# Two-layer Perceiver on one core: split first chunk and PSUM maxima in the last cross-attention head, other filler counts, and a reordered expert loop

## The chip, the cores and the metric

The kernel runs on one core of a Trainium2 chip. The metric is the time of one execution in device microseconds (us), lower is better; the figure that counts is the median of several executions. A core has five engines with queues of their own: PE (matrix products, results in PSUM), DVE (VectorE, elementwise and reductions), ACT (ScalarE, activations and copies), POOL (GpSimd, which here also issues some transfers) and SP (SyncE, which only issues transfers). They wait for each other through semaphores, and each runs its own instructions in order.

## The reference, cut to what matters

`x` is 256 tokens by 512, `ctx` 4096 by 512. Six residual steps follow one another, each on a layernorm of `x`:

```python
x = x + xattn0(ln(x), ctx)      # 16 heads of 128, 4096 keys
x = x + attn0(ln(x))            # 16 heads of 32, q, k, v rounded to e4m3
x = x + ffn0(ln(x))             # relu MLP plus a gated expert
x = x + xattn1(ln(x), ctx)      # keeps the 54 largest scores of a token
x = x + attn1(ln(x))            # 16 heads of 32, biases
x = x + moe(ln(x))              # 64 experts, top 8, at most 64 tokens each
```

The cross-attention and the last step, where most of the change lies:

```python
scores = einsum('bqhd,bkhd->bhqk', q, k); attn = softmax(scores)
ctx_out = einsum('bhqk,bkhd->bqhd', attn, v) @ Wo
h = silu(xg @ w1.T) * (xg @ v1.T)      # per expert, F = 192
y = h @ w2;  out = scatter_add(weight * y)
```

## The kernel before, in words

Every engine has one function per step, and the order of work on each is written out by hand. There is no scheduler; the order in the code is the order in the queue.

**Cross-attention.** A head's 4096 keys are worked through in 8 chunks of 512 (`NCH`), numbered over all heads as `n = h * NCH + j`; `TAIL` is the first chunk of the last head. Per chunk PE makes scores into the two-bank PSUM tile `twin`, ACT copies them into `S` in SBUF (`store_scores`), DVE keeps a running maximum (`keep_max`). After the last chunk DVE folds it (`L692`), POOL takes the maximum over partitions (`largest_score`, L896) into `mrow`. Then, per chunk, DVE subtracts (`shift`, L699), ACT takes the exponential (`raise_scores`, L539) and rounds it to a high part (`round_e`, L548), DVE makes the low part (`split_e`, L719), and PE multiplies both with the values (`weigh`, L403, and for the last head the sums, L408). The parts have two places, so `round_e` of a chunk waits until the chunk two before it is weighed. In all heads but the last this lies beside the projection of the next head's keys. In the last head there is nothing beside it, and `stay_awake` (L135), products into a bank that nobody reads, fills PE's wait. POOL also loads the values back from HBM in `load_v`.

**Attentions.** `tensor_attention` works in four groups of four heads: scores, maxima on DVE (`maxima`, L1262), the negated maxima split in three and turned (L1049), scores turned (L1062, L1066), exponential on ACT (L1199), sums and products (`weigh_group`, L1084, L1092), `normalise` on DVE, and at the end `project_out(i, c)` (L1099) for token tile `i` and group `c`. In the first attention q, k and v are quantised on DVE before (L1255 ends q and k each). It calls `stay_awake` 30 times before the first scores.

**Experts.** Two experts make a pair, 32 pairs, two pairs a couple `q`, four pairs a group. Weights lie in a ring of 7 pairs (2304 KB each); SP refills a place once `hid_down` says that the couple is done. For the first group the tokens are gathered by products (`gather`); for the later ones `find_gates(g)` yields the token numbers of the group, `gpsimd_rows` fetches the rows by an indirect transfer (L1854), and `turn_rows` transposes them into `GATHER_B` (L1915), from which ACT copies (`move_rows`). Then `up` (L1930), silu on ACT, `make_hid` on DVE, `turn` (L1943), `move_hid` on DVE, `down` (L1954, L1958), `round_y` on ACT, `split_y` and `make_selT` on DVE and `spread_out` (L1968) into the two output banks. A loop pass of PE is: up, gates of the next group (every other pass), up, turn rows, down, two spreads, turn, turn rows.

## Time and profile before

| | |
|---|---|
| runs | 1680.07 us median of 3 (1679.98 to 1680.2) |
| the profiled execution | 1675.72 us, its span 1673.9 us |
| PE busy | 1624.5 us, 97% of the span, 9280 products |
| DVE, ACT, POOL busy | 1076.1, 695.1, 127.0 us |
| transfers | 270.40 MB, mean 162 GB/s |
| TensorE's granted clock | 0.996 on average over the span |

The profile is one execution, so durations and gaps are those of 1675.72 us, 4.35 us under the median of the runs. Busy PE includes the filler products. The cross-attention ends at about 1180 us of the span, the first attention at about 1250, the experts start at about 1456.

### The profile page before, as it was taken

The page shows a single profiled execution, that of the slowest core. Times are in us where ns is not written, and L with a number is a line of the kernel's source. Part 1 is how long each engine was busy: PE and PEld are TensorE (multiplying, and loading weights), DVE is VectorE, ACT ScalarE, POOL GpSimd, SP SyncE. Part 2 cuts the span into 40 slices and gives each one's busy share as a digit, 9 for nine tenths or more (in the row PEclk, how much of TensorE's full clock was granted, in tenths as well). Part 3 has the DMA queues.
Part 4 walks back from the last instruction along what each step waited for, and adds up shares of the span by engine and source line. Part 5 has one row for each costly group of instructions (what it writes and reads, how often), then busy time and mean ns, then how long its engine had stood idle before and what let it go on. Part 6 is the DMA issues. An engine that isn't in the chain of part 4 may idle for free.

```text
span 1673.9 us, 23515 instructions
## 1 busy us (share of the span) xinstructions
PE 1624.5 (97%) x9280; PEld 1285.7 (77%) x9280; DVE 1076.1 (64%) x1706; ACT 695.1 (42%) x938; POOL 127.0 (8%) x212
## 2 busy tenths in 40 slices
PE   8998999999999999999999999999979999999998
PEld 7887888888788888878888888888747746554444
DVE  4445777777777777777777779998473842633333
ACT  3334544454444444454454546665231321322222
POOL 0000000000000000000000010111000000011110
PEclk9999999999999999999999999999989999999999
DMA  6755445554454545545544552325210517479994
GB/s 225 202 173 167 123 130 141 130 133 116 140 140 127 133 127 132 132 139 139 135 131 118 139 147 92 108 95 193 91 54 30 201 51 304 171 208 426 422 422 174
DMA packets 117292, 270.40 MB, mean 162 GB/s; under 512 B 7168, under 2 KB 76992, under 8 KB 111040
## 3 DMA queue, kind: packets, MB, share of 16 engines
q1 hardware_dynamic: 96512, 194.45, 36.7%
q0 software_dynamic: 20672, 74.46, 14.5%
q8 instruction: 74, 1.21, 0.3%
q14 instruction: 34, 0.28, 0.0%
HBM read 200.69 MB, written 68.19 MB: 161 GB/s over the span
## 4 chain that ended last, share of the span: by engine, by line
PE 71%; issue 16%; DVE 6%; DMA 3%; ACT 2%; POOL 2%; SPq 0%; DVEq 0%; POOLq 0%; ACTq 0%
PE bank L390 16%; PE bank L41 16%; PE bank L362 12%; PE bank L403 7%; PE bank L1930 4%; PE bank L1554 3%; PE bank L1968 2%; PE bank L1954 2%; DMA v_dram<-v_out 1%; DVE e_lo L719 1%; PE bank L135 1%; PE bank L428 1%; PE bank L1958 1%; POOL v_back L890 1%; PE bank L1915 1%
## 5 line engine op out<-in xcount | busy, mean ns | idle before, releaser
L719 DVE TENSOR_TENSOR e_lo<-S,e_hi 128x1024 fp32r<-128x1024 f32 x128 | 156.6, 1224 | 89.3 <-ACT e_hi L548 88.7
L362 PE MATMUL bank<-cT_hi,wk_hi 128*128 128x512 f32 x512 | 205.4, 401 | 0.0
L390 PE MATMUL bank<-wv_hi,cT_hi 128*128 128x512 f32 x512 | 199.8, 390 | 3.4 <-DVE wv_lo L656 3.4
L539 ACT ACTIVATE S<-S 128x1024 f32<-128x1024 f32 x128 | 135.6, 1059 | 160.2 <-DVE S L699 159.6
L362 PE MATMUL bank<-cT_hi,wk_lo 128*128 128x512 f32 x512 | 200.6, 392 | 0.0
L390 PE MATMUL bank<-wv_hi,cT_lo 128*128 128x512 f32 x512 | 199.4, 390 | 0.0
L362 PE MATMUL bank<-cT_lo,wk_hi 128*128 128x512 f32 x512 | 199.2, 389 | 0.0
L390 PE MATMUL bank<-wv_lo,cT_hi 128*128 128x512 f32 x512 | 199.2, 389 | 0.0
L548 ACT CAST e_hi<-S 128x1024 fp32r<-128x1024 f32 x128 | 134.7, 1052 | 139.6 <-PE bank L403 135.1
L712 DVE TENSOR_TENSOR esum<-esum,S 128x512 f32<-128x512 f32 x210 | 145.0, 691 | 71.1 <-ACT S L539 67.5
L403 PE MATMUL bank<-e_hi,v_back 128*128 128x256 f32 x880 | 167.0, 287 | 5.3 <-DVE e_lo L719 3.5
L687 DVE TENSOR_TENSOR mx<-mx,S 128x512 f32<-128x512 f32 x224 | 154.4, 689 | 14.3 <-ACT S L533 10.4
L699 DVE TENSOR_TENSOR S<-S,mrow 128x1024 f32<-128x1024 f32 x128 | 155.3, 1216 | 3.2 <-POOL mrow L896 3.2
L41 PE MATMUL bank<-q_hi,k_hi 128*128 128x256 f32 x512 | 145.4, 284 | 10.2 <-DVE k_lo L674 10.2
L403 PEld LDWEIGHTS bank<-e_hi,v_back 128*128 128x128 f32 x880 | 138.8, 191 | 9.5 <-issue 7.9
L41 PE MATMUL bank<-q_lo,k_hi 128*128 128x256 f32 x512 | 144.8, 283 | 0.0
L41 PE MATMUL bank<-q_hi,k_lo 128*128 128x256 f32 x512 | 144.8, 283 | 0.0
L519 ACT CAST k_hi<-bank 128x512 fp32r<-128x512 f32 x128 | 75.3, 588 | 155.2 <-PE bank L362 155.2
L533 ACT COPY S<-bank 128x1024 f32<-128x1024 f32 x128 | 128.7, 1006 | 11.1 <-PE bank L41 11.1
L890 POOL DMA_DIRECT2D v_back<-v_dram x110 | 59.0, 537 | 868.0 <-PE bank L403 832.0
L403 PE MATMUL bank<-e_lo,v_back 128*128 128x256 f32 x440 | 124.4, 283 | 0.0
L724 DVE TENSOR_TENSOR v_out<-bank,v_out 128x512 fp32r<-128x512 f32 x112 | 76.9, 687 | 59.9 <-ACT v_out L555 59.9
(279 smaller groups left out, 2805.2 us busy)
## 6 DMA issues: line engine op xcount, KB each, us to landing
w<-in_w_moe SPq DMA_DIRECT2D x32, 2304.0 KB, 17.5
v_dram<-v_out SPq DMA_DIRECT2D x112, 512.0 KB, 4.6
v_back<-v_dram POOLq DMA_DIRECT2D x110, 512.0 KB
v_dram<-v_back SPq DMA_DIRECT2D x16, 512.0 KB, 3.9
ctx_nat<-in_ctx SPq DMA_DIRECT2D x8, 1024.0 KB, 4.9
ctx_raw<-in_ctxT SPq DMA_DIRECT2D x7, 1024.0 KB, 8.0
v_late<-v_dram POOLq DMA_DIRECT2D x14, 512.0 KB
l_w_qkv<-in_l_wqkv SPq DMA_DIRECT2D x6, 1024.0 KB, 5.5
```

What stands on the lines that cost most here:

```text
L41: last = e.matmul(dst, lhs, rhs, start=(n == 0), stop=(n == len(terms) - 1))
L362: t = e.matmul(banks[b][:], l, r, start=(c == 0 and m == 0), stop=(c == DT - 1 and m == 2))
L390: t = e.matmul(banks[b][:], l, r, start=(c == 0 and m == 0), stop=(c == DT - 1 and m == 2))
L403: t = e.matmul(banks[O_BANK][:, 0:T], v[:, i, l, :], r[:, i, :], start=(j == 0 and i == 0 and m == 0), stop=(j == NCH - 1 and i == CT - 1 ...
L533: e.copy(S[:, j * CT:(j + 1) * CT, :].rearrange("p a t -> p (a t)"), twin[:]).then_inc(s_stored, 1)
L539: e.activation(Sj, Sj, ACT.Exp).then_inc(raised, 1)
L548: e.copy(e_place(n)[0][:], S[:, j * CT:(j + 1) * CT, :]).then_inc(e_rounded, 1)
L687: own.done(e.tensor_tensor(mx[:], mx[:], two, ALU.max))
L699: e.tensor_tensor(Sj, Sj, mrow[:].unsqueeze(1).to_broadcast([P, CT, T]), ALU.subtract).then_inc(shifted, 1)
L712: e.tensor_tensor(esum[:], esum[:], two, ALU.add).then_inc(e_summed, 1)
L719: e.tensor_tensor(lo[:], Sj, hi[:].bitcast(F32), ALU.subtract).then_inc(e_split, 1)
L724: e.tensor_tensor(place_of[:, :, 1, :].bitcast(F32R), banks[b][:].rearrange("p (q d) -> p q d", q=HPQ), place_of[:, :, 0, :].bitcast(F32), ...
```

## The change

**Last head of the cross-attention.** DVE folds the first seven chunks' maxima while PE still makes the last scores, reduces the last chunk straight from `twin`, and joins the two (`keep_last_max`). ACT stores the last scores only behind that. Chunk `TAIL` goes through shift, exponential, rounding and split in two halves (`HALVES`), and PE's `weigh` starts on the first. The sum fold and the ones matrix move behind the maxima, `add_head` of the head before goes from the middle of the loop to its end, each `shift` goes ahead of the split before it. POOL issues the loads of chunks `TAIL` + 2 and + 3, then the maximum, then the load of `TAIL` + 1. `weigh` of the very last chunk signals once behind the products and once behind the sums. The filler goes from 18 calls to 6.

**First attention.** 30 calls become 19; 3 are added between the two parts of the first scores, 7 ahead of the second and third group's scores, and the 4 ahead of the turned maxima of three groups go. In both attentions token tile 0 has its four output products before tile 1's second.

**Experts.** The filler of the router goes from 10 calls to 3 in the second tile and from 7 to 2 behind the ranks. `gather` waits for each half of the selection. Gates go into the bank of the second y instead of `GATHER_B`, so `find_gates` waits for `y_split` and `down` for `gates_moved`. The first passes are written out: `down(0)` comes ahead of `turn_rows(4)`. In the later passes `turn_rows(2q+2)` stands ahead of the second `up` (and, in passes with gates, right behind them). The last `down` comes behind three more spreads and DVE moves hid first in the last pass. The output tile 0 is added before tile 1's last spread is done.

```diff
@@ tensor_cross
-            stay_awake(e, banks[K_BANK], 18)
+            stay_awake(e, banks[K_BANK], 6)
@@ scalar_cross
             h = XH - 1
+            move_o(h - 1)
             store_scores(h, NCH - 1)
-            move_o(h - 1)
-            for j in range(NCH):
+            for m in HALVES:
+                raise_scores(h, 0, m)
+                round_e(h, 0, m)
+            for j in range(1, NCH):
                 raise_scores(h, j)
                 round_e(h, j)
             move_o(h)
             e.wait_ge(sum_ready, h)
+            e.wait_ge(weighed, NH + 1)
@@ vector_cross
+            def keep_last_max():
+                own.wait(e)
+                e.wait_ge(max_ready, XH - 1)
+                own.done(e.tensor_reduce(mxr[:], mx[:].rearrange("p a t -> p t a"), AX.X, ALU.max))
+                own.wait(e)
+                e.wait_ge(scored, NH)
+                own.done(e.tensor_reduce(mx[:, 0, :], twin[:].rearrange("p (a t) -> p t a", t=T), AX.X, ALU.max))
+                own.wait(e)
+                e.tensor_tensor(mxr[:], mxr[:], mx[:, 0, :], ALU.max).then_inc(max_folded, 1)
...
             h = XH - 1
+            keep_last_max()
+            fold_sum(h - 1)
             own.done(e.tensor_scalar(ones_r[:], ident[:], 0.0, 1.0, ALU.mult, ALU.add))
-            fold_sum(h - 1)
-            keep_max(h, NCH - 1)
             own.wait(e)
-            shift(h, 0)
+            for m in HALVES:
+                shift(h, 0, m)
+            invert_sum(h - 1)
             shift(h, 1)
-            invert_sum(h - 1)
-            for j in range(NCH):
+            for m in HALVES:
+                split_e(h, 0, m)
+            for j in range(1, NCH):
+                if j + 1 < NCH:
+                    shift(h, j + 1)
                 split_e(h, j)
-                if j == NCH // 2:
-                    add_head(h - 1)
-                if j + 2 < NCH:
-                    shift(h, j + 2)
+            add_head(h - 1)
@@ gpsimd_cross
-                        for ahead in (1, 2, 3):
-                            load_v(n + ahead)
+                        load_v(n + 2)
+                        load_v(n + 3)
+                        largest_score(h)
+                        load_v(n + 1)
@@ tensor_attention
-                if k == 0 and f < 3:
-                    stay_awake(e, turned_bank(0), 4)
...
-                stay_awake(e, W_BANK, 30)
+                stay_awake(e, W_BANK, 19)
                 e.wait_ge(quant_done, 2)
                 scores(0, (0, 1, 2))
+                stay_awake(e, W_BANK, 3)
                 scores(0, (3,))
...
+                    if f < 2 and k == 0:
+                        stay_awake(e, W_BANK, 7)
                     scores(f + 1, (0, 1, 2))
...
             project_out(0, 1)
-            project_out(1, 1)
             project_out(0, 2)
             project_out(0, 3)
+            project_out(1, 1)
             project_out(1, 2)
@@ tensor_moe
-                stay_awake(e, banks[5], 2 + 8 * i)
+                stay_awake(e, banks[5], 2 + i)
...
-            stay_awake(e, GATHER_B, 7)
+            stay_awake(e, GATHER_B, 2)
...
+            up(0)
+            find_gates(1)
+            up(1)
+            up(2)
+            turn(0)
+            up(3)
+            down(0)
+            turn_rows(4)
+            turn(1)
+            turn_rows(5)
+            for q in range(2, COUPLES):
+                up(2 * q)
+                if q % 2 == 0 and q // 2 + 1 < NG:
+                    find_gates(q // 2 + 1)
+                if 2 * q + 2 < PAIRS:
+                    turn_rows(2 * q + 2)
+                up(2 * q + 1)
+                down(q - 1)
+                if q == COUPLES - 1:
+                    turn(q)
+                spread_out(2 * q - 4)
+                spread_out(2 * q - 3)
+                if q < COUPLES - 1:
+                    turn(q)
+                    turn_rows(2 * q + 3)
+            spread_out(PAIRS - 4)
+            down(COUPLES - 1)
+            for p in range(PAIRS - 3, PAIRS):
+                spread_out(p)
@@ scalar_moe
+                    silu(2 * q)
+                    if q > 1 and 2 * q + 2 < PAIRS:
+                        move_rows(2 * q + 2)
+                    silu(2 * q + 1)
+                if q == 1:
+                    move_rows(4)
                 if q:
                     round_y(2 * q - 2)
+                if q == 1:
+                    move_rows(5)
+                if q:
                     round_y(2 * q - 1)
```

## Rows read from the trace of the kernel before

**Rows 1.** Chain that ended last (start us, us, what), end of the last head

```profile
1176.52 0.38 ACT oT L561
```

**Rows 2.** Timeline, last head (start, us, engine, line, operation, count, idle before)

```profile
1147.95 0.69 DVE L692 TENSOR_REDUCE mxr<-mx 128x256 f32<-128x512 f32 x1
...
1148.98 1.03 POOL L896 PARTITION_ALL_REDUCE mrow<-mxr  x1
...
1150.11 2.36 DVE L699 TENSOR_TENSOR S<-S,mrow 128x1024 f32<-128x1024 f32 x2 [1.46 <-POOL mrow L896]
...
1152.51 1.05 ACT L548 CAST e_hi<-S 128x1024 fp32r<-128x1024 f32 x1
...
1153.59 1.23 DVE L719 TENSOR_TENSOR e_lo<-S,e_hi 128x1024 fp32r<-128x1024 f32 x1 [1.04 <-ACT e_hi L548]
...
1168.73 0.48 PE L403 MATMUL bank<-e_hi,v_late 128*128 128x256 f32 x2 [0.96 <-DVE e_lo L719]
```

**Rows 3.** Timeline, first attention

```profile
1211.02 1.23 DVE L1255 SCALAR_TENSOR_TENSOR l_k<-l_xn,l_qkT 128x1024 bf16<-128x1024 f32 x1
...
1214.84 1.89 DVE L1262 TENSOR_REDUCE l_mx<-bank 128x2 f32<-128x512 f32 x3 [1.46 <-PE bank L1037]
...
1229.06 1.94 PE L1084 MATMUL bank<-l_eT,ones 128*32 128x256 f32 x16
...
1235.39 1.07 PE L1084 MATMUL bank<-l_eT,ones 128*32 128x256 f32 x16
```

**Rows 4.** Windows of the first attention (PE, PEld, DVE, ACT, POOL busy, PEclk, DMA, GB/s)

```profile
1214.40:1217.50 3.10, 0.70 (x8) 0.14 (x8) 2.60 (x8) 0.30 (x1) 0.00 (x0) 1.00 0.80 327
1217.50:1224.40 6.90, 4.32 (x37) 2.88 (x40) 6.59 (x13) 4.41 (x7) 0.00 (x0) 0.50 0.01 3
```

**Rows 5.** Timeline, end of the second attention and the router

```profile
1449.96 5.42 PE L1099 MATMUL bank<-l_w_out,xT 128*128 128x512 f32 x12
1451.12 0.42 DVE L1287 SCALAR_TENSOR_TENSOR xT<-bank,l_inv 128x256 f32<-128x256 f32 x1
...
1459.14 2.45 PE L135 MATMUL bank<-ident 128*128 128x128 f32 x20
...
1459.79 1.04 ACT L2034 CAST xn_hi<-xn 128x1024 fp32r<-128x1024 f32 x1 [0.23 <-DVE xn L123]
```

**Rows 6.** Waits of PE from 1470 us to the end (total us, times, longest)

```profile
PE bank L1954 <- DVE hidT L2108: 1.9, 1, 1.9
PE bank L1915 <- DMA rows<-xn_dram,ids: 1.4, 1, 1.4
PE bank L1943 <- DVE h L2101: 1.0, 1, 1.0
PE bank L1968 <- DVE selT L2087: 0.9, 1, 0.9
PE bank L41 <- DVE sel L2064: 0.6, 1, 0.6
```

**Rows 7.** One group of four pairs, as a window

```profile
1572.28:1596.61 24.33, 24.33 (x144) 12.02 (x146) 8.45 (x24) 6.01 (x12) 3.79 (x4) 1.00 1.01 424
```

**Rows 8.** Chain that ended last, in the expert step

```profile
1649.81 5.31 PE bank L1930 x32
...
1662.10 1.94 PE bank L1954 x8
1664.03 1.02 PE bank L1958 x8
...
1667.99 2.09 PE bank L1968 x8
...
1670.10 0.69 DVE x L2167
```

**Rows 9.** The tile rows6, from 1476 us to the end: issues and landings

```profile
L1854 POOL DMA_INDIRECT rows<-xn_dram,ids x28: 943/947/1189, 1477.7 to 1626.9; - x28
...
DMA to landing us min/median/max: 8.7/11.8/13.1
```

More of the change, by code:

```diff
@@ L226, in k_before, with of_chunk, reached @@
             return n if n <= LATE * NCH + NCH else n - 1 if n > LATE * NCH + NCH + 1 else 0
+        HALVES = (0, 1)
+        def of_chunk(j, m=None):
+            return slice(j * CT, (j + 1) * CT) if m is None else slice(j * CT + m * CT // 2, j * CT + (m + 1) * CT // 2)
+        def reached(n, m=None):
+            return n + 1 + (n > TAIL or n == TAIL and m != 0)
         def e_place(n):
@@ L397, in weigh @@
                 e.wait_ge(landed_v, value)
-                e.wait_ge(e_split, n + 1)
+                e.wait_ge(e_split, n + 1 if n <= TAIL else reached(n))
                 if j == 0 and h:
@@ L401, in weigh @@
                 for i in range(CT):
+                    if n == TAIL and i == CT // 2:
+                        e.wait_ge(e_split, reached(n))
                     for m, (l, r) in enumerate(((0, high), (1, high), (0, low))):
@@ L404, in weigh @@
                                      start=(j == 0 and i == 0 and m == 0), stop=(j == NCH - 1 and i == CT - 1 and m == 2))
+                if n == NH - 1:
+                    t.then_inc(weighed, 1)
                 if h == XH - 1:
@@ L910, in gpsimd_cross @@
                     elif n == TAIL:
[L911 to L912 removed]
+                        load_v(n + 2)
+                        load_v(n + 3)
+                        largest_score(h)
+                        load_v(n + 1)
                     elif n + 3 < NH:
                         load_v(n + 3)
[L915 removed]
+                    if h and j == 0 and n != TAIL:
                         largest_score(h)
@@ L1008, in sync_attention @@
                 if k == 0:
-                    e.wait_ge(e_split, NH - NCH + 2 * n + 2)
+                    e.wait_ge(e_split, reached(TAIL + 2 * n + 1))
                 else:
@@ L1887, in gather @@
                 if c == 0:
-                    e.wait_ge(sel_made, TT)
                     e.wait_ge(xn_split, 1)
                 cols = slice(c * P, (c + 1) * P)
-                matmuls(e, gather_bank(c), [(xn[:, i, cols], sel[:, 0, i, :]) for i in range(TT) for xn in (xn_hi, xn_lo)]).then_inc(gathered, 1)
+                for i in range(TT):
+                    if c == 0:
+                        e.wait_ge(sel_made, i + 1)
+                    for part in (xn_hi, xn_lo):
+                        t = e.matmul(gather_bank(c), part[:, i, cols], sel[:, 0, i, :], start=(i == 0 and part is xn_hi),
+                                     stop=(i == TT - 1 and part is xn_lo))
+                t.then_inc(gathered, 1)
             def find_gates(g):
@@ L1901, in find_gates @@
                     e.wait_ge(gates_moved, 3 * g)
-                    e.wait_ge(xg_moved, DT + GROUP * (g - 2) + 2 if g > 1 else DT)
+                    e.wait_ge(xg_moved, DT)
+                    if g > 1:
+                        e.wait_ge(y_split, GROUP * (g - 1) - 2)
                 for n in range(GROUP):
@@ L1969, in spread_out @@
                                      start=(p == 0 and part is y_hi), stop=(p == PAIRS - 1 and part is y_lo))
+                    if p == PAIRS - 1 and i == 0:
+                        t.then_inc(spread, 1)
                 t.then_inc(spread, 1)
@@ L2020, in move_rows, with silu @@
                 e.copy(xgT[:, p % 2].rearrange("p c s -> p (c s)"), GATHER_B).then_inc(xg_moved, 1)
+            def silu(p):
+                e.wait_ge(hid_up, p + 1)
+                if p >= 2:
+                    e.wait_ge(hid_made, 2 * (p - 1))
+                e.activation(sa[:, p % 2, :], banks[UP_BANKS[p % 2]][:, 0:FF], ACT.Silu).then_inc(hid_silu, 1)
             def round_y(p):
@@ L2161, in vector_moe @@
                 if q < COUPLES:
-                    move_hid(q)
+                    if q not in (0, COUPLES - 1):
+                        move_hid(q)
                     if q % 2 and q // 2 + 2 < NG:
                         make_sel(q // 2 + 2)
-            e.wait_ge(spread, PAIRS)
             for i in range(TT):
+                e.wait_ge(spread, PAIRS + i)
                 e.tensor_tensor(x[:, i, :], banks[OUT_BANKS[i]][:], x[:, i, :], ALU.add).then_inc(y_added, 1)
```

64 lines of the change are left out of this document (23 added, 41 removed).

## The prediction

> **What bounds the kernel now.** I read the shares of the page first: PE is busy 97% of the span, so a gain can only come from PE's waits and from busy time that is filler. Then the chain of waits, to see which stretches are not plain PE work, then the timeline of those stretches, then the waits of PE by releaser. The reader is to see that the change leaves the long loop of heads alone (span 0 to 1142) and works on four places where PE waits or fills: the last head, the first attention, the router, and both ends of the expert loop. In the middle of the expert loop PE is busy all 24.33 us of a group of four pairs [rows 7]; nothing is to be had there, and the transfers run beside it at full share too.
>
> **Last head.** Before, ACT stores the last scores (1.0), DVE takes them in two steps of 0.7 and folds from 1147.95 to 1148.64, so the scores themselves end at about 1145.45; POOL reduces from 1148.98 to 1150.01, because its three loads hold it until then [rows 2]. After: DVE folds the first chunks beside the last scores, then reduces `twin`. The trace has no reduction of 1024 columns; one of 512 takes 0.69 in SBUF [rows 2] and three from PSUM take 1.89, 0.63 each [rows 3]. By twice 0.63 it takes 1.25; were PSUM read with a stride of 256 twice as slow, 2.5; and 0.63 is the least that half the columns take, so no gain is below that. I take 1.25, since the PSUM rows, which read in a straight line, show no extra. The join is 256 columns, 0.35 by half of 0.69. Maximum ready at 1145.7 + 1.25 + 0.35 = 1147.35, POOL done at 1148.45. DVE has by then folded the sums and made the ones. Shift in halves (0.6 each, half of 2.36 for two [rows 2] and again halved): the first is out at 1149.15. ACT's four halves, 0.55 to 0.6 each by halves of 1.05, end at 1151.7; DVE's split of the first half waits for its own `shift(h, 1)` until 1151.2 and ends at 1151.85. PE starts there instead of at 1154.9, when the split of 1153.59 was done [rows 2]: 3.0 earlier. PE's filler: the fold of the sums is later now, so PE's output products end at 1150.55, and 6 calls of 0.22 (20 products, 10 calls, 2.45 [rows 5]) end at 1151.9. Filler and wait match; 18 calls would have held PE until 1154.6.
> The second chunk gives 0.9 back: its rounding stands behind the four halves, its split ends at 1155.2, PE would be free at 1154.3. From there both kernels go by the same circle, a chunk weighed, rounded 1.05, split 1.22, two chunks in 5.1. `add_head` inside the loop made a wait of 0.96 [rows 2]; at the end it is hidden by the last products. 3.0 - 0.9 + 1.0 = 3.1, and I find 0.3 more where the restarts of PE fall away: 3.4. The early signal lets ACT move `oT`, 0.38 [rows 1], beside the sums: 0.4. **3.8** in all. The load of chunk `TAIL` + 1 moves behind POOL's reduction, 1.4 later; it is wanted only at 1155.2, 6.7 after its issue.
>
> **First attention.** DVE is free at 1213.4 and waits 1.46 for the first scores, PE being in its filler until about 1214.4, although k was ready at 1212.25 (1211.02 + 1.23) [rows 3]. 11 calls less end at 1211.9, so PE waits for k and DVE starts 1.45 earlier. From here I followed each engine's list with the durations of the trace. Where it wins most is behind the second split of maxima: before, the filler of 4 calls stood between the maxima and their turning and took 2.07 because the clock had fallen; the 7 calls now stand ahead of scores that wait for DVE anyway. The sums of the first group (1229.06 before) start at 1225.4 and, at full clock, last 1.07 instead of 1.94; those of the second group (1235.39 before) start at 1230.6 [rows 3]. That is 4.7, with the clock up.
> The clock is the open term. Before, PE was busy 0.70 of 3.1 us, at full clock, and the stretch that follows has 0.50, 1.2 GHz [rows 4]. In the new order PE is busy some 0.8 of 3.6 us between the second filler and the turned scores, about as little. With the whole stretch at 1.2 GHz my lists give 2.6 instead of 4.7. I take **4.0**, between, since the new order has one such thin place and the old one had several.
> The Trainium skill speaks against taking filler away ("TensorE: Matmul & The Clock Gate", on the clock gate: throttled is the default state and activity lifts it). By it the fall would remain and the 2.6 stand; the trace shows the fall in the same place, and cannot show the new order.
>
> **Output order.** Six products take 5.42, 0.9 each [rows 5]. Tile 0's last is the third instead of the fourth, starts at 1449.96 + 1.8 = 1451.8, and its input is moved at 1451.54 [rows 5]: not late. DVE's add, norm and all behind it come 0.9 earlier, in both attentions: **1.8**. Tile 1's end is the same 5.42, and DVE comes to it later than that.
>
> **Router.** Tile 1 is normalised at 1459.76, but the 10 calls hold PE until 1461.4; ACT is free for the move at 1460.83 [rows 5]. With 3 calls the move starts there instead of at 1462.06: 1.2. With `gather` starting on the first half of the selection (the filler of 7 would cover that start, 2 don't) two products of 0.23 are done before the second half: 0.5. **1.7.** PE stays busy for most of this stretch, so I expect no fall of the clock; if it fell over the gather, 16 products of 0.23 would double, 3.6.
>
> **Start of the experts.** PE waits 1.0 for the first hid, 1.4 for the first row transfer, 0.6 for the third selection [rows 6]. Written out, up(1) and up(2) cover the first wait. From the gates of group 1: three ups (half of 5.31 each), a turn of 0.33, `down` 1.94 + 1.02 [rows 8]: 11.4 us, and the rows landed 10.9 behind these gates. So `down(0)` ends 3.1 earlier. But now both row moves of ACT stand ahead of the two roundings of y, so split, selection and `find_gates(2)` end later behind `down(0)`: I get 1.2 of waiting there (0.6 before), and 0.4 for rows 5. `down(1)` starts 1.3 earlier. Bounds: all three waits gone, 3.0; rows late, 0. I take **1.3**. The Trainium skill says that transfers of all issuing engines run on the same 16 DMA engines and interleave ("DMA: Bandwidth & Descriptors", Issuing engines are not separate DMA queues). By it the weights that `down(0)` now releases earlier would share with rows 5 to 7, which before had landed by then, and the term would go towards 0.
>
> **In the loop.** The gates bank is free in time (the y of that bank is split before the selection is made), so that wait costs nothing; without that cover it is one split, 0.7. A group's first row is wanted earlier: from the end of `find_gates` 14.3 before, 11.7 now, one up less. Gates moved and issued take 1.0 and landing 8.7 at least, 11.8 in the median, 13.1 at most [rows 9]. The group's first is issued into the least queue, and the first of group 1 took 9.4, so 10.4 < 11.7: nothing.
>
> **End of the experts.** From the end of the last up (1655.12) to the end of the adds (1671.5) 16.4 [rows 8]. PE waits 1.9 and 0.9 [rows 6]. After: down(14), turn, two spreads of 1.02 until 5.1, spread(28) from 5.75 (its y rounded and split), down(15) from 6.75 to 9.7, spread(29), then spread(30) from 11.45 and (31) to 13.5, each behind rounding 0.6, split 0.7, selection 0.3. The first add starts half a spread earlier; adds end at 14.4: **2.0**.
>
> **Sum.** 3.8 + 4.0 + 1.8 + 1.7 + 1.3 + 2.0 = 14.6. Nothing else of the span changes its order, and the transfers of the later steps are issued by signals that move along. The profiled execution's 1675.72 (span 1673.9 and 1.8 around it) becomes 1661.1; the runs are 4.35 above it, which I keep: 1680.07 - 14.6 = **1665.5**.
>
> **The rivals.** (a) The clock: it stays at 1.2 GHz through the first attention, and falls once more where filler was taken. For it: the thin stretch [rows 4]. Against: the head's and router's fillers shrink only by waits. 14.6 - 1.4 - 3.6 = 9.6, 1670.5; with the first alone 1666.9. (b) The reduction from PSUM is slow and the start of the experts gives nothing, because the rows share with the weights: 14.6 - 1.25 - 1.3 = 12, and waits that my lists miss (each engine's list has some twenty hand-overs of 0.04) take 3 more: 1671. (c) Slower: rows of a group's first pair too late. PE then stands still once per group, in six groups. Each us that the landing takes over 10.7 costs 6 us. At the median 11.8 it costs 6.6, 1672; at 13.1, 14.4, and all is lost, 1680; slower from 13.8 on. For it: the loop's transfers are at full share [rows 7]; against: only the later rows of a group queue behind others. (d) The fillers were never on the path, and only the reordering counts: 1.45 and 1.2 go, 1668.
>
> **How the numbers follow.** Forecast with (d) and the milder half of (a) 0.73, the rest of (a) 0.10, (b) 0.08, (c) 0.09, of which 0.03 beyond no change. 0.2% is 3.4 us, about what a measurement of this kernel can tell from no change. Low: all waits at the start gone (+1.7) and the clock up (+0.7) give 1663.1, and I leave 0.6 for smaller ones; high: 1671.5 takes in (b) and the larger (a). Faster 0.94, same 0.03, slower 0.03.
>
> **What would show it.** PE's first product of the last head near 1152 and the move of `oT` ahead of the last sums; the reduction from `twin` at 1.25; granted clock of the first attention's stretch; `down(0)` ending before row 4 is turned; a wait of PE for the selection of about 1.2, and none at L1915 in the later groups. I am wrong if L1915 waits for rows six times, or if a new stretch has 0.50.

## The result, and the profile after

The changed kernel takes 1664.01 us (median of 4 runs, 1663.39 to 1668.64), against 1680.03 us (4 runs, 1677.14 to 1680.2) for the kernel before on the same chip: a ratio of 0.9915, 95% interval 0.9894 to 0.9935, so faster by 10.9 to 17.8 us. The forecast was 1665.5 (range 1662.5 to 1671.5): faster, as forecast, 1.5 us beside the number. Run again beside experiments 5, 6 and 8 the changed kernel gave 1664.65 (6 runs) against 1679.33 (11 runs) for the kernel before, 14.7 us less.

The profiled execution took 1663.39 us. Top of its page, span and busy time by engine:

```profile
span 1661.6 us, 23410 instructions
PE 1619.7 (97%) x9220; PEld 1281.3 (77%) x9220; DVE 1076.4 (65%) x1708; ACT 695.5 (42%) x940; POOL 126.8 (8%) x212
```

The busy share tells nothing of the change: PE was 97% busy before too, with its filler counted in. So the account is made by stages, each from the start of one instruction to the start of another that both kernels have (the last one to the end of the adds), from the two profiled executions (us):

| stage | before | after | gain |
|---|---|---|---|
| last `v_back` load to the last maximum on POOL | 5.84 | 4.39 | 1.45 |
| from there to the first `rstd` of the next norm on POOL | 32.77 | 30.50 | 2.27 |
| first attention (third reduction of `l_sc` to the next norm's first `rstd`) | 36.61 | 33.89 | 2.72 |
| from there to the first norm behind the second attention | 205.60 | 204.75 | 0.85 |
| router (second norm to the first issue of rows) | 19.12 | 17.16 | 1.96 |
| start of the experts (to `find_gates(2)`) | 17.20 | 15.98 | 1.22 |
| five periods of a group | 5 x 24.33 | 5 x 24.09 | 1.2 |
| last `find_gates` to the end of the adds | 54.83 | 53.29 | 1.54 |

Together 13.2. The spans differ by 12.3, since the long loop, which no edit touches, happened to be 0.91 longer in the execution of after. Over the 14 kernels profiled here the last `v_back` load stands anywhere from 1143.14 (the kernel before) to 1147.82, with the same code ahead of it. The execution of before that the prediction was read from was the quickest of all in that stretch. Part of the wandering is the clock: in the first 160 us of the span it was at 0.50 for no time in two of them (before, and experiment 10), for 3.4 us in seven and for 6.8 us in five; the load stands at 1143.14 and 1144.42 in these two, at 1144.05 to 1145.82 with 3.4 us, and at 1145.40 to 1147.82 with 6.8. The medians differ by 16.0, more than the two spans; what the executions without a trace did in that loop isn't known, so I compare stages from here on.

**Last head.** Timeline, as in [rows 2]:

```profile
1146.66 1.23 DVE L722 TENSOR_REDUCE mx<-bank 128x256 f32<-128x1024 f32 x1
...
1147.92 0.42 DVE L724 TENSOR_TENSOR mxr<-mxr,mx 128x256 f32<-128x256 f32 x1
...
1148.44 1.07 POOL L931 PARTITION_ALL_REDUCE mrow<-mxr  x1 [0.58 <-DVE mxr L724]
...
1149.61 1.29 DVE L733 TENSOR_TENSOR S<-S,mrow 128x512 f32<-128x512 f32 x2 [0.48 <-POOL mrow L931]
...
1151.33 1.50 PE L135 MATMUL bank<-ident 128*128 128x128 f32 x12
...
1152.81 0.47 PE L416 MATMUL bank<-e_hi,v_back 128*128 128x256 f32 x2
...
1156.41 0.47 PE L416 MATMUL bank<-e_hi,v_late 128*128 128x256 f32 x2 [0.79 <-DVE e_lo L752]
```

The reduction of `twin` takes 1.23 (1.25 was estimated), the join 0.42 (0.35). The filler ends at 1152.83, about where the first half of the first chunk is ready (1152.70): PE's first product is 3.0 us earlier than in [rows 2] when the 0.9 of the loop is taken out. The second chunk gives back 0.79 (0.9 was estimated), and the wait of 0.96 behind `add_head` in [rows 2] is gone. The output products start 0.44 us behind the last sums before and right behind them after, because `oT` is moved beside the sums (0.4 was estimated).

**First attention.** Timeline, as in [rows 3]:

```profile
1210.48 1.88 DVE L1300 TENSOR_REDUCE l_mx<-bank 128x2 f32<-128x512 f32 x3
...
1216.43 3.25 PE L135 MATMUL bank<-ident 128*128 128x128 f32 x14
...
1219.96 0.39 PE L1074 MATMUL bank<-l_k,l_q 32*128 32x256 bf16 x6 [0.28 <-DVE l_mx L1300]
...
1222.43 1.58 PE L1119 MATMUL bank<-l_eT,ones 128*32 128x256 f32 x16
...
1229.08 1.40 PE L1119 MATMUL bank<-l_eT,ones 128*32 128x256 f32 x16
```

DVE's first reduction no longer waits (1.46 before). But 7 calls of filler, 14 products, take 3.25 us, where 14 took 1.83 a little earlier in the same stretch (1211.54), and the sums of groups 0 and 1 take 1.58 and 1.40 instead of 1.07 [rows 3]. The windows say why (us, busy PE, PEld, DVE, ACT, POOL with instructions, granted clock, DMA share, GB/s):

```profile
1212.62:1216.03 3.41, 1.97 (x32) 1.28 (x31) 3.24 (x10) 2.56 (x3) 0.00 (x0) 1.00 0.46 183
1216.03:1219.44 3.41, 3.41 (x20) 3.03 (x15) 3.27 (x5) 2.42 (x4) 0.00 (x0) 0.50 0.00 0
1219.44:1222.86 3.42, 2.11 (x36) 1.09 (x39) 3.28 (x9) 0.90 (x2) 0.00 (x0) 1.00 0.00 0
1222.86:1226.27 3.41, 3.41 (x35) 1.30 (x28) 1.55 (x6) 1.90 (x4) 0.00 (x0) 0.50 0.00 0
1226.27:1229.68 3.41, 1.76 (x32) 0.90 (x36) 3.38 (x5) 2.42 (x5) 0.00 (x0) 1.00 0.00 0
1229.68:1233.10 3.42, 3.42 (x29) 1.37 (x18) 2.37 (x7) 0.38 (x1) 0.00 (x0) 0.50 0.02 5
```

Where before the clock fell once, for 13.65 us, it now falls three times for 3.4 us each, to 1.2 GHz, each time behind a stretch in which PE was busy 1.8 to 2.1 of 3.4 us. Of the two new fillers of 7 calls, the one ahead of the scores of group 1 runs at full clock (1.83), the one ahead of group 2's at the low clock (3.25); the thin places are ahead of it, around the turning of the maxima. The third of these pieces is a new one: it covers the values of group 1 and output products, which ran at full clock in the kernel before.

**End of the first attention and of the kernel, and the start of the experts.** The chain, end of the first attention, before and after:

```profile
1244.43 3.65 PE bank L1099 x8
...
1239.76 2.79 PE bank L1134 x6
...
1242.64 0.70 DVE x L1376
```

Six instructions, 2.79, stand on it after, where the chain of the kernel before has eight, 3.65. The trace records each output product as two instructions, so that is three products and four. Waits of PE from 1468 us to the end, as in [rows 6]:

```profile
PE bank L2012 <- DVE selT L2154: 1.5, 2, 0.9
PE bank L41 <- DVE sel L2131: 1.1, 1, 1.1
PE bank L1958 <- ACT xgT L2079: 0.4, 1, 0.4
PE bank L1958 <- DMA rows<-xn_dram,ids: 0.2, 1, 0.2
```

The waits for `h` (1.0), for the first row transfer (1.4) and for the last `hidT` (1.9) are gone; the wait for `sel` is longer (1.1, was 0.6), and one of 0.4 for `xgT` is new. Both were forecast, at 1.2 and 0.4. The rows are waited for once, 0.2, and in no later group. Issues and landings of the rows, as in [rows 9]:

```profile
L1892 POOL DMA_INDIRECT rows<-xn_dram,ids x28: 941/947/1189, 1469.4 to 1615.9; - x28
...
DMA to landing us min/median/max: 7.8/9.5/12.5
```

**In the loop** something was gained that nobody had counted. The chain over one couple:

```profile
1581.80 0.98 PE bank L41 x8
1582.78 0.52 PE bank L1958 x4
1583.30 2.73 PE bank L1973 x16
1586.03 1.72 PE bank L1998 x8
```

The first eight products of `down` take 1.72 on the chain, right behind an `up`. In the kernel before they stand behind the four turnings of a row and take 1.87 there; only the one behind the last `up`, with no turning between, takes 1.72:

```profile
1572.28 1.87 PE bank L1954 x8
...
1655.12 1.72 PE bank L1954 x8
```

### The profile page after: what moved, and what is told of

It is laid out like the page before. It is cut to its first block, busy times and chain, and to the rows that moved or that the text cites. A ratio compares the mean times of both kernels' runs of the same rounds, so it can differ in the third digit from the quotient of the medians.

```text
span 1661.6 us, 23410 instructions
## 1 busy us (share of the span) xinstructions
PE 1619.7 (97%) x9220; PEld 1281.3 (77%) x9220; DVE 1076.4 (65%) x1708; ACT 695.5 (42%) x940; POOL 126.8 (8%) x212
## 3 DMA queue, kind: packets, MB, share of 16 engines
q0 software_dynamic: 20672, 74.46, 14.7%
## 4 chain that ended last, share of the span: by engine, by line
PE 70%; issue 18%; DVE 4%; DMA 3%; ACT 2%; POOL 2%; SPq 0%; POOLq 0%; DVEq 0%; ACTq 0%
PE bank L401 17%; PE bank L41 15%; PE bank L373 13%; PE bank L416 7%; PE bank L1973 5%; PE bank L1592 3%; PE bank L2012 2%; PE bank L1998 2%; DMA v_dram<-v_out 1%; POOL v_back L925 1%; PE bank L2002 1%; PE bank L443 1%; PE bank L1958 1%; DMA v_out<-in_wv 1%; DMA rows<-xn_dram,ids 1%
## 5 line engine op out<-in xcount | busy, mean ns | idle before, releaser
L752 DVE TENSOR_TENSOR e_lo<-S,e_hi 128x1024 fp32r<-128x1024 f32 (+1 forms) x129 | 156.8, 1215 | 88.9 <-ACT e_hi L565 88.3
L556 ACT ACTIVATE S<-S 128x1024 f32<-128x1024 f32 (+1 forms) x129 | 135.8, 1053 | 154.2 <-DVE S L733 153.7
L565 ACT CAST e_hi<-S 128x1024 fp32r<-128x1024 f32 (+1 forms) x129 | 134.9, 1046 | 140.8 <-PE bank L416 136.1
L733 DVE TENSOR_TENSOR S<-S,mrow 128x1024 f32<-128x1024 f32 (+1 forms) x129 | 155.4, 1207 | 2.2 <-POOL mrow L931 2.2
## 6 DMA issues: line engine op xcount, KB each, us to landing
w<-in_w_moe SPq DMA_DIRECT2D x32, 2304.0 KB, 14.7
```

The lines of the kernel that those rows point to most:

```text
L556: e.activation(Sj, Sj, ACT.Exp).then_inc(raised, 1)
L565: e.copy(e_place(n)[0][:, of_chunk(0, m), :], S[:, of_chunk(j, m), :]).then_inc(e_rounded, 1)
L733: e.tensor_tensor(Sj, Sj, mrow[:].unsqueeze(1).to_broadcast([P, CT if m is None else CT // 2, T]), ALU.subtract).then_inc(shifted, 1)
L752: e.tensor_tensor(lo, S[:, of_chunk(j, m), :], hi.bitcast(F32), ALU.subtract).then_inc(e_split, 1)
```

## The experiments

Milestones are those of the table above.

**1. Only the last head.** The kernel before with the hunks of the cross-attention alone:

```
+            keep_last_max()
+            fold_sum(h - 1)
...
+            for m in HALVES:
+                shift(h, 0, m)
...
-            stay_awake(e, banks[K_BANK], 18)
+            stay_awake(e, banks[K_BANK], 6)
```

> The kernel before with the part of the last cross-attention head alone. Theory: the terms add up stage by stage, so this part is worth 3.7 us (between the last scores and the first add of head 15, measured 1179.50 against 1176.69 with the earlier loop taken out), PE's first product of the last head comes about 9.5 us behind the start of the last scores instead of 12.4, and everything behind keeps its old distances: about 1676.3 in the runs. Rival: the gain is partly given back in the first attention, because the clock falls at another point of it; then the distance from the last head to the end of the first attention changes by 1 us or more though its code is that of before.

Measured: 1676.11 (10 runs) against 1679.03 (21 runs), ratio 0.9978 (0.9969 to 0.9988). The two stages of the head are 4.38 and 30.50, as in the full change: 3.7 gained. Of that 1.7 is lost again in the next stage (33.41 instead of 31.72), where the clock stood at 1.2 GHz for 3.4 us at 1184 in this execution, which it does in none of the other kernels; so the rival came true here, in one execution. The attention, whose code is that of before, took 37.00. The head's term holds.

**2. Only the fillers of the first attention.**

```
-                stay_awake(e, W_BANK, 30)
+                stay_awake(e, W_BANK, 19)
...
+                stay_awake(e, W_BANK, 3)
...
+                        stay_awake(e, W_BANK, 7)
...
-                if k == 0 and f < 3:
-                    stay_awake(e, turned_bank(0), 4)
```

> The kernel before with the filler counts of the first attention alone (30 to 19, 3 and 7 and 7 added, 4 taken three times). Theory: DVE starts the first maxima 1.5 us earlier, and the stretch up to the end of the first attention is shorter by 1.8 us, because the clock still falls in it: about 1678. Rival A, as the prediction had it: 4.0. Rival B, the clock stays up and it is 4.7: about 1675.3. The granted clock between 1214 and 1240 us of the span tells them apart (0.5 for 10 to 14 us in all by the theory, 1.0 by rival B).

Measured: 1676.82 (10 runs), ratio 0.9977 (0.9964 to 0.9991). The stage takes 34.89 instead of 36.61: 1.7, less than either figure of the prediction (4.7 with the clock up, 2.6 down). It is 2.1 to 2.4 against the same stage in experiments 1 and 3, whose attention is also that of before. The clock falls three times for 3.4 us, at 1221.2, 1228.0 and 1234.8, the pattern of the full change.

**3. Only the router and the experts.** The kernel before with the hunks from `gates_place` on, the new order among them:

```
+            up(0)
+            find_gates(1)
+            up(1)
+            up(2)
+            turn(0)
+            up(3)
+            down(0)
+            turn_rows(4)
...
```

> The kernel before with the change of the expert step alone (router filler, gather, gates bank, written out start, rows behind gates, end). Theory: 1.8 for the router, 1.5 for the start, 1.3 for the loop, 1.3 for the end, 5.9 in all, about 1674.2; a group of four pairs takes 24.09 instead of 24.33. Rival: the loop gain is not of this order but of the transfers, and depends on when they start; then the group takes 24.33 here.

Measured: 1673.11 (6 runs), ratio 0.996 (0.9947 to 0.9973). Router 17.33 (1.8 gained), start 15.53 (1.7), group 24.09 (0.24 each), last part 53.29 (1.5). The attention is untouched: 37.26, clock down for 13.65 us. So the stage of the unchanged attention took 36.61, 37.00 and 37.26 in three executions: the later the fall begins in it (4.0, 4.8 and 5.4 us behind the third reduction of `l_sc`), the longer it is. With the changed attention it took 33.76 to 34.23 in seven (the changed kernel twice, and 5 and 9 to 12).

**4. The clock kept up.** The changed kernel with more filler where the thin places are, all of it where PE waits:

```
+                if k == 0 and f < 2:
+                    stay_awake(e, W_BANK, 2)
                 e.wait_ge(as_negs, 4 * k + f + 1)
...
+                if k == 0 and f < 2:
+                    stay_awake(e, W_BANK, (3, 2)[f])
+                if k == 0 and f == 2:
+                    e.wait_ge(as_raised, base + SHG * f)
+                    stay_awake(e, turned_bank(1), 2)
...
-                        stay_awake(e, W_BANK, 7)
+                        stay_awake(e, W_BANK, (7, 13)[f])
```

> The changed kernel with more filler in the waits of the first attention (2 calls ahead of the turned maxima of the first two groups, 3, 2 and 2 between these and the turned scores, 13 instead of 7 ahead of the third group's scores). Theory: the 2.9 us by which the first attention fell short of 4.7 are the three stretches at 1.2 GHz; if the filler keeps the clock up, the sums of the second group come 4.5 us or more after those of the first as before, PE's sums last 1.07 instead of 1.4 to 1.9, and the kernel is 2 to 3 us faster than the changed one, about 1661. Rival: the filler itself is in the way, the clock falls all the same, and it is slower than the changed kernel by 0 to 3 us.

Measured: 1662.95 (4 runs), ratio 0.99 (0.9884 to 0.9917). The stage takes 30.85 instead of 33.89, 3.0 us less, and the clock stays at 2.4 GHz. Windows:

```profile
1212.00:1216.00 4.00, 3.83 (x34) 3.10 (x32) 3.79 (x13) 2.55 (x3) 0.00 (x0) 1.00 0.71 287
1216.00:1220.00 4.00, 3.94 (x44) 3.49 (x44) 3.86 (x6) 2.43 (x5) 0.00 (x0) 1.00 0.00 0
1220.00:1224.00 4.00, 3.47 (x55) 2.42 (x58) 3.75 (x10) 1.54 (x4) 0.00 (x0) 1.00 0.00 0
1224.00:1228.00 4.00, 2.64 (x46) 1.41 (x38) 3.54 (x8) 3.00 (x7) 0.00 (x0) 1.00 0.01 4
```

And its timeline, sums and values of group 0:

```profile
1222.93 1.07 PE L1126 MATMUL bank<-l_eT,ones 128*32 128x256 f32 x16
1223.82 1.05 PE L1134 MATMUL bank<-l_eT,l_v 128*32 128x256 f32 x16
```

This shows the cause of the missing gain: same work, same order, more filler, and the sums are back at 1.07. Counted from the third reduction of `l_sc`, the scores of group 2 start at 9.3 in both kernels; the sums of groups 0, 1 and 2 start at 11.78, 18.42 and 24.57 in the changed one and at 11.70, 17.02 and 21.52 here. So the first of the three falls costs 0.1 at most, though it makes a filler nearly twice as long; the other two, which lie over sums, values and output products, cost 1.3 and 1.65. Against the kernel before the filler term is now 36.61 - 30.85 - 0.9 (for the output order) = 4.9; 4.7 had been worked out for a clock that stays up. The medians differ by 1.1 (1662.95 against 1664.01) while the profiled spans differ by 2.6 and the stage by 3.0; with 4 runs of each, the intervals of the two ratios overlap, so it is the stage that shows it, not this total; it came out 1.1 below the changed kernel and not the 2 to 3 that were expected. Experiment 8, measured on one chip with the changed kernel, bears the stages out.

**5. Rows turned behind the couple again.** The changed kernel, `turn_rows(2q + 2)` back behind `up(2q + 1)`, and ACT's move with it:

```
-                if 2 * q + 2 < PAIRS:
-                    turn_rows(2 * q + 2)
                 up(2 * q + 1)
+                if 2 * q + 2 < PAIRS:
+                    turn_rows(2 * q + 2)
                 down(q - 1)
```

> The changed kernel with the transposes of row 2q+2 behind the second up again, ahead of down, in the passes from q = 2 on (and ACT's copy of them behind the second silu). Theory: the 0.24 us per group of four pairs that the loop gained come from what stands next to what on PE (down lasts 1.72 behind an up and 1.87 behind transposes), so the group takes 24.33 again and the kernel is 1.4 us slower than the changed one. Rival: they come from the gates bank or the transfers; then the group stays at 24.09.

Measured: 1665.16 (6 runs), against 1664.65 for the changed kernel on the same chip: 0.5, inside the noise of the medians, where 1.4 was expected. The group is 24.33 again, to the last digit that of before, and the last part 53.53 instead of 53.29; together 1.4 longer. The chain over one couple:

```profile
1583.91 2.73 PE bank L1973 x16
1586.64 0.59 PE bank L1958 x4
1587.22 1.87 PE bank L1998 x8
```

Behind the turnings `down` takes 1.87, behind an `up` 1.72. The 0.24 of a group is twice 0.15 for `down`, and 0.07 and 0.01 for the turnings (0.52 and 0.58, both 0.59 before), less 0.15 for two `up` that no longer stand side by side (2.73 twice, against 5.31 for the 32 products together in [rows 8]).

**6. Without the new filler.** The changed kernel without the calls of 3 and of 7:

```
-                stay_awake(e, W_BANK, 3)
...
-                    if f < 2 and k == 0:
-                        stay_awake(e, W_BANK, 7)
```

> The changed kernel without the 3 calls between the first scores and the 7 and 7 ahead of the second and third group's scores in the first attention; the 19 calls stay. Theory: the new filler is what lifted the clock between its falls; without it the clock stays at 0.5 for 13.7 us in one piece and the stretch from the third POOL reduction of the quantisation to the first root of the next norm is 1 to 2 us longer than the 33.89 of the changed kernel. Rival: the filler is dead weight, because it runs while the clock is down at 0.45 us a call, and the stretch is shorter without it.

Measured: 1666.41 (5 runs); the stage takes 34.56, 0.7 more than in the first execution of the changed kernel and 0.3 to 0.8 more than in the seven; 1 to 2 was expected. Windows:

```profile
1211.40:1214.81 3.41, 0.95 (x10) 0.23 (x8) 3.41 (x6) 0.00 (x0) 0.35 (x1) 0.99 1.01 418
1214.81:1228.46 13.65, 7.67 (x80) 3.41 (x84) 11.19 (x28) 7.77 (x12) 0.00 (x0) 0.50 0.13 52
```

The clock stays down for 13.65 us in one piece, as before, and falls once more for 3.4 us at 1231.82. The stage is still 1.2 quicker than that of the kernel before once the output order's 0.9 is taken out (36.61 - 34.56 - 0.9). So by these executions 1.1 of the 1.8 that the filler hunks bring comes from taking 30 to 19 and the three calls of 4 away, and 0.7 from the filler put in. With one execution here, and a stage that varies by 0.5 and more from one execution to the next, the shares are rough. That both are gains is likely: 34.56 lies between the two ranges, 35.7 to 36.4 (the old filler, with 0.9 taken off for the output order) and 33.76 to 34.23.

**7. The changed kernel again**, on the chip of 5, 6 and 8.

> The changed kernel once more, on the chip of the others. Expected 1663 to 1665; the clock falls in the first attention again, in pieces of 3.4 us, and the stretch there is 33 to 35 us. If the clock falls at other places in every execution, this run shows by how much the stretch varies without any change of code.

Measured: 1664.65 (6 runs, 1662.51 to 1669.6), ratio 0.9914 (0.9899 to 0.993). All stages of its profiled execution repeat within 0.15, and the clock falls at the same three places of the attention.

**8. A better kernel.** Experiment 4, and DVE's list in the expert step turned at two places:

```
+                if q == 1:
+                    make_sel(2)
...
+                        if q >= COUPLES - 1:
+                            make_selT(p)
+                            split_y(p)
+                        else:
+                            split_y(p)
+                            make_selT(p)
```

> The changed kernel with the filler of the first attention as in e4_warm, with the third selection made ahead of the first splits of y (DVE idles 3.7 us there, and PE waited 1.1 for that selection), and with the last four selT made ahead of their split of y (0.34 us each, two of them on the path). Expected: clock at 1.00 in the first attention, no wait of PE for sel, 1.1 + 0.6 us less than e4_warm, 2.6 to 4.7 less than the changed kernel, about 1660.5. Rival: the start of the expert loop then waits for rows 6 and 7 or for the weights instead, and only 0.6 of the 1.7 is seen.

Measured: 1659.93 (4 runs, 1658.67 to 1662.12), ratio 0.9881 (0.9866 to 0.9896): 4.7 below the changed kernel on the same chip, 19.4 below the kernel before. By stages it is 4.9 below experiment 7: 2.9 in the attention, where the clock stays at 2.4 GHz, 1.3 at the start and 0.65 at the end. So here the total shows what the clock is worth too. The start of the experts takes 14.56 (1.2 to 1.4 below those of 4 and of the change), the last part 52.64 (0.65 below). Waits of PE from 1468 us to the end:

```profile
PE bank L2019 <- DVE y_lo L2188: 0.8, 2, 0.5
PE bank L1965 <- ACT xgT L2086: 0.4, 1, 0.4
```

The wait for `sel` is gone, since the third selection is made before the splits of y; the 1.5 at the end has become 0.8, since the expanded selection is made while ACT still rounds y.

**9 to 12. The last head taken apart**, one execution each beside one of the kernel before (1677.06). The times are 1664.70, 1665.81, 1664.47 and 1668.63; differences are read from the stages.

9: the first chunk whole instead of in halves.

```
-        HALVES = (0, 1)
+        HALVES = (None,)
```

> The changed kernel with the last head's first chunk in one piece again instead of halves. Read on the stretch from the last POOL reduction of the heads to the first root of the next norm, 30.49 to 30.51 us in seven executions. Theory: the halves bring PE's first product 0.7 us earlier, but the second chunk then waits for ACT's four halves (PE waited 0.79 there), so the stretch is longer by 0 to 0.3 us. Rival, as the prediction counted: the early start is kept, and it is longer by 0.6 or more.

10: the filler back at 18 calls.

```
-            stay_awake(e, banks[K_BANK], 6)
+            stay_awake(e, banks[K_BANK], 18)
```

> The changed kernel with 18 filler calls in the last head again. Theory: they end at 4.0 instead of 1.5 us behind the output products, 2.5 us behind the start of the first chunk's products, of which 0.8 fall into the wait ahead of the second chunk: the stretch from the last POOL reduction to the next root is 1.5 to 1.8 us longer than 30.50. Rival: filler is never on the path; it stays at 30.5.

11: the last addition of a head back in the middle.

```
+                if j == NCH // 2:
+                    add_head(h - 1)
...
-            add_head(h - 1)
```

> The changed kernel with add_head of the head before in the middle of the last head's loop again. Theory: the wait of 0.96 us that it made before comes back, the stretch is 31.5. Rival: with the shift ahead of the split DVE has room for it, and it stays at 30.5.

12: maxima of the last scores from their copy in SBUF again.

```
-            keep_last_max()
             fold_sum(h - 1)
+            keep_max(h, NCH - 1)
...
-                if n == NH - 1:
-                    e.wait_ge(max_folded, XH)
```

> The changed kernel with the last chunk's maximum taken from the stored scores by two steps and one fold again, behind the fold of the sums; POOL's order stays as changed. Read from the last load of v_back to the last POOL reduction, 4.38 to 4.42 us in seven executions, 5.8 before. Theory: the store (1.0), two steps (1.4) and the fold (0.7) against 1.23 and 0.42: 5.5, as POOL's loads no longer hold the reduction (0.3 of the 1.45 gained). Rival: the loads were the whole reason, and it stays near 4.4.

Measured, as time from the last `v_back` load to the maximum, and from there to the norm (4.39 and 30.50 after): 9: 4.39 and 30.91. 10: 4.41 and 32.43. 11: 4.39 and 31.36. 12: 7.30 and 31.05. Timeline of 10, where PE comes out of its filler 2.6 after the split of the first half:

```profile
1151.72 4.18 PE L135 MATMUL bank<-ident 128*128 128x128 f32 x36
1155.66 0.48 PE L416 MATMUL bank<-e_hi,v_back 128*128 128x256 f32 x2
```

Timeline of 9, where the wait stands at the first chunk:

```profile
1155.23 0.47 PE L416 MATMUL bank<-e_hi,v_back 128*128 128x256 f32 x2 [1.58 <-issue]
```

In 9 PE begins 1.6 later (6.0 behind the maximum instead of 4.4) and the stage ends only 0.4 later, between the theory (0 to 0.3) and the rival (0.6 or more). The second chunk's products start 8.44 behind the maximum instead of 7.97, the last chunk's 23.81 instead of 23.34: of the 1.6, 0.5 is left at the second chunk, where PE's wait of 0.79 is gone, and it stays so to the end, as each later chunk comes out of the circle of ACT and DVE. Splitting a chunk in halves buys its start, and little of its end. In 10, 2.5 later at the start is 1.9 at the end (1.5 to 1.8 was expected). In 11 the addition costs 0.86, and the row shows it:

```profile
1167.69 0.47 PE L416 MATMUL bank<-e_hi,v_late 128*128 128x256 f32 x2 [0.95 <-DVE e_lo L752]
```

In 12 the maximum is 2.9 later than after, where 1.1 was expected, and also 1.5 later than in the kernel before (5.84), which takes it from SBUF too. Timeline of 12:

```profile
1149.56 0.37 ACT L576 COPY oT<-bank 128x256 f32<-128x256 f32 x1 [4.42 <-PE bank L416]
1149.83 1.02 ACT L548 COPY S<-bank 128x1024 f32<-128x1024 f32 x1
...
1150.88 1.42 DVE L706 TENSOR_TENSOR mx<-mx,S 128x512 f32<-128x512 f32 x2 [2.60 <-ACT S L548]
```

The store of the scores stands behind the move of the head before's `oT`, which waits for that head's last products; DVE waits 2.6 for it. Putting this move ahead of the store had no term in the prediction (its 0.4 is for the `oT` of the last head). No cost of it shows where the maxima come from PSUM, and by these rows it is what makes 12 later than the kernel before. Two edits of the same change hang together. The next stage of 12 holds another fall of the clock: 3.4 us at 0.50 from 1158.90, behind 3.4 us in which PE was busy for 1.42. So the 31.05 isn't comparable with the 30.50.

## Why the prediction was right, step by step

| term | forecast | measured | by |
|---|---|---|---|
| last head | 3.8 | 3.7 | stages; alone 3.7 (experiment 1) |
| fillers of the first attention | 4.0 | 1.8 | stage less 0.9; alone 1.7 (2); 1.5 to 2.6 over all executions of both |
| output order, twice | 1.8 | 1.75 | 0.85 in the second, 0.9 in the first |
| router | 1.7 | 1.96 | stage; alone 1.8 (3) |
| start of the experts | 1.3 | 1.2 | stage; alone 1.7 (3); 1.2 to 1.7 over all executions |
| in the loop | 0 | 1.4 | 0.24 in each of six groups (3, 5) |
| end of the experts | 2.0 | 1.3 | last `up` to the end of the adds: 16.27, 14.96 |

**The sum** was 14.6 and came out at 13.2 by stages and at 14.7 and 16.0 by medians. The nearness owes something to luck: the attention and the end were 2.9 too high (2.6 with the mean of all executions of the attention), and the loop, at which I had put nothing, returned 1.4 of that. The 0.9 of the first attention's output order had no experiment of its own: it is 3.65 less 2.79 on the two chains, and fits the stage's 2.72 less the 1.72 of experiment 2, which has the old order and 3.65 on its chain. ("Six products take 5.42" in the prediction counts products of the kernel; the row has them as x12.)

**The last head** went by the lists: reduction, join, PE's restart, the second chunk's wait and the early `oT` each came within 0.15. Two sums were a little off: a call of filler is 0.245 by the row that was cited (2.45 for ten), not 0.22, and six took 1.50; and 1145.7 + 1.25 + 0.35 is 1147.30. What I had not worked out is how little a start is worth once the second chunk stands behind four halves (9): the term came from PE's rows from start to end, so the sum held all the same.

**The first attention** is the step that was mis-sized, and the clock is why. The prediction gave 4.7 with the clock up, 2.6 with it down, and took 4.0, "since the new order has one such thin place and the old one had several". The rows say three: PE was busy 1.97, 2.11 and 1.76 of some 3.4 us, and behind each the clock was 0.50. I had looked for a stretch as empty as that of [rows 4], 0.70 of 3.1; the clock fell behind stretches with more than twice that. Experiment 4 settles it: the clock kept up, 4.9 come. The 2.6 for the low clock was high too: 1.8 by the first pair of executions, 2.1 by the means of all (36.96 and 33.99), and only the extremes (37.26 and 33.76) give 2.6. The filler of 7 calls that takes 3.25 at the low clock has no part in that. In experiments 10 and 12 the first fall didn't come, that filler took 1.83, and PE then waited for DVE; rows of 10:

```profile
1218.57 1.83 PE L135 MATMUL bank<-ident 128*128 128x128 f32 x14
1222.27 0.39 PE L1074 MATMUL bank<-l_k,l_q 32*128 32x256 bf16 x6 [1.87 <-DVE l_mx L1300]
```

The scores behind it start 9.3 us after the third reduction of `l_sc` with the fall and without, and the stage, 34.23 and 34.01, is no shorter. What costs is a low clock over the sums, the values and the output products. By its own sign ("I am wrong ... if a new stretch has 0.50") the prediction was wrong on this term: the third piece is such a stretch. The rule that I set against my figure, that the clock is low by default and activity lifts it (the Trainium skill, "TensorE: Matmul & The Clock Gate", What's actually happening), pointed the right way: the fall remained. I had given it too little weight.

**Rival (a)**, the clock, thus came true for the most part in its first half (three pieces, 10.2 us in all, and not the whole attention) and not in its second: router and gather ran at full clock. **Rival (c)**, rows too late, did not: one wait of 0.2, and landings of 9.5 in the median, below the 11.8 of [rows 9]. Whether they land sooner because they are asked for at another point of the weights' stream wasn't tried. **Rival (b)** fell with the reduction's 1.23. **Rival (d)**, that only the reordering counts, is refused for the head by experiment 10 (12 calls less are worth 1.9) and for the attention by 2 and 6: the filler hunks bring 1.7 alone, of which removing brings about 1.1. In the router filler and `gather` were not parted. The rule that the transfers of all issuing engines share the same DMA engines (the Trainium skill, "DMA: Bandwidth & Descriptors", Issuing engines are not separate DMA queues) would have taken the start's term towards 0; no run here tells whether they interleave so, but the term came as 1.2 with one wait of 0.2 for rows. (Three ups, a turn and `down` add up to 11.26, not to 11.4, and took 11.3.)

**The loop.** "A group of four pairs ... nothing is to be had there" was wrong: a busy PE can be sped up by what stands next to what. The row was there, in the trace of before: the `down` of 1.72 behind the last `up` (1655.12).

**The end** was 0.7 too high. `down` for the last couple starts 7.1 behind the last `up`, not 6.75: rounding, split and selection take 1.8 from the product to the product that waits for them, where I had added up 1.6, and PE stands there twice (0.9 and 0.6). The last spreads and adds take 3.2 instead of 2.95, and 0.1 is in my reading of the time before, 16.4 for 16.27. Experiment 8 gets 0.65 of it back by turning that list.

## What to carry to other kernels

Size filler by what PE does between the fillers, not by the length of one wait: here 10.2 us of attention kept 1.2 GHz in three pieces until the gaps around the small products were filled too, and that was worth 3.0 us, more than the 1.1 for removing filler that was too long. Ask what the low clock lies over: over a filler that ends in a wait it cost nothing, over the sums and values 1.3 us and more. Follow a saved microsecond to the end of its stage: 1.6 us at the start of PE was 0.5 at the second chunk and 0.4 at the end. And compare stages between fixed instructions when the total wanders: the unchanged loop varied by 4.7 us between executions, more than any term of this sum.

## What the runs showed of the hardware

- DVE reduces 1024 columns of PSUM, read at a stride of 256, in 1.23 us; 512 columns in a straight line take 0.63. No cost of the stride shows: 1.23 is less than twice 0.63.
- The granted clock fell behind stretches in which PE was busy 1.8 to 2.1 of 3.4 us with 32-row and bf16 products, and came back 3.4 us later; with less filler (experiment 6, 0.95 of 3.41 ahead of the fall) it stayed down for 13.65 us. PE's longest idle time in the changed kernel's attention was 1.2 us. Busy time alone doesn't tell a fall from none: in experiment 10, with the same code, PE was busy 1.98 of 3.41 us (1214.56 to 1217.97) and the clock stayed at 1.00.
- The same eight products take 1.72 us on the chain behind the 128x384 products of `up` and 1.87 behind four 128x128 transposes, and 16 products of `up` 2.73 alone while 32 take 5.31. So what stands beside a group of products changes its time on these chains by up to 0.15 us; why isn't shown.
- Over 14 executions with the same code up to there, the last `v_back` load came at 1143.14 to 1147.82 us, later in the executions with more time at 0.50 early in the span (none: 1143.14 and 1144.42; 6.8 us: 1145.40 to 1147.82).
